# Router's GELU inside the attention loop, early logits and choices spread over group 7, the last four batches last

## The reference

```
x = x + tanh(g_xattn) * attention(layernorm(x), ctx)       # 16 heads of 16, causal
xf = layernorm(x); ri = concat(xf, six statistics of each row)
h = gelu(ri @ r1_w.T + r1_b); probs = softmax(h @ r2_w.T)  # 32 experts
top 2 of each token; each expert takes its 140 best tokens
x = x + tanh(g_ffn) * (experts' output, weighted + 16 shared adapters)
```

## Time and profile before

| | |
|---|---|
| median of 3 runs | 810.26 us (809.97 to 812.16) |
| profiled execution: its own time, its span | 806.49 us, 804.7 us |
| PE, DVE, ACT, POOL busy | 675.4, 507.6, 393.2, 322.9 us |
| mean granted PE clock | 0.914 of full |
| chain that ended last | PE 60%, DVE 17%, ACT 14% |

### The profile page before, as it was taken

How to read it: one execution, slowest core, us unless ns; L and a number is a source line. 1 busy time by engine, 2 the same in 40 slices (tenths; PEclk the granted TensorE clock), 3 DMA queues, 4 the chain that set the end, 5 groups by cost and what they waited for, 6 DMA issues and landing times.

```text
span 804.7 us, 17481 instructions
## 1 busy us (share of the span) xinstructions
PE 675.4 (84%) x5198; PEld 532.4 (66%) x5198; DVE 507.6 (63%) x1371; ACT 393.2 (49%) x1590; POOL 322.9 (40%) x339
## 2 busy tenths in 40 slices
PE   7899999999999999998866111079999999999993
PEld 4456666666666666665643100069999999999992
DVE  5665777867777786766578888925454545454541
ACT  1467686867768686777732563012222222222220
POOL 3343453534445353441101000035656565656542
PEclk8999999999999999999976555579999999999997
DMA  5600020202002020101014200018898988898931
GB/s 163 238 1 24 25 70 2 70 26 69 24 23 70 2 69 24 46 1 46 2 41 133 74 1 0 0 33 258 245 274 253 266 243 272 251 274 234 278 60 14
DMA packets 57422, 84.44 MB, mean 105 GB/s; under 512 B 11282, under 2 KB 28304, under 8 KB 57360
## 3 DMA queue, kind: packets, MB, share of 16 engines
q1 hardware_dynamic: 47168, 73.04, 27.7%
q0 software_dynamic: 9216, 9.76, 7.4%
q10 hardware_dynamic: 976, 0.96, 0.4%
HBM read 71.04 MB, written 12.69 MB: 104 GB/s over the span
## 4 chain that ended last, share of the span: by engine, by line
PE 60%; DVE 17%; ACT 14%; issue 4%; DMA 2%; SPq 1%; POOL 1%; ACTq 0%; DVEq 0%; POOLq 0%
PE pair L808 19%; PE bank L818 10%; ACT arena L1083 7%; PE pair L1385 6%; DVE arena L1254 5%; PE pair L1394 3%; PE bank L1413 3%; PE bank L1352 3%; PE pair L1380 3%; DVE arena L669 3%; PE bank L1340 2%; PE bank L1345 2%; PE bank L828 2%; ACT arena L489 2%; PE bank L1364 1%
## 5 line engine op out<-in xcount | busy, mean ns | idle before, releaser
L1083 ACT ACTIVATE arena<-pair,arena 112x112 f32<-112x112 f32 x512 | 175.5, 365 | 72.3 <-DVE arena L1254 68.5
L808 PE MATMUL pair<-arena,we 128*128 128x140 f32 x1024 | 139.9, 285 | 0.7 <-ACT arena L729 0.6
L772 DVE SCALAR_TENSOR_TENSOR arena<-arena,pair 128x140 f32<-128x140 f32 x160 | 47.7, 298 | 133.8 <-issue 73.6
L714 POOL DMA_INDIRECT rows_out<-arena,slot_row x64 | 94.4, 1475 | 92.7 <-DVE arena L761 75.0
L808 PEld LDWEIGHTS pair<-arena,we 128*128 128x128 f32 x1024 | 130.1, 192 | 1.8 <-issue 1.8
L737 ACT ACTIVATE arena<-pair 128x140 f32<-128x140 f32 x160 | 45.9, 287 | 149.0 <-PE pair L808 99.0
L705 POOL DMA_INDIRECT arena<-rows,slot_row x64 | 62.5, 977 | 120.8 <-issue 120.8
L1083 ACT ACTIVATION_READ_ACCUMULATOR arena<-pair,arena 112x1 f32 x512 | 110.0, 215 | 0.0
L818 PE MATMUL bank<-arena,we 128*128 128x140 f32 x512 | 83.3, 286 | 0.0
L1254 DVE TENSOR_REDUCE arena<-pair 112x8 f32<-112x896 f32 x64 | 69.4, 1085 | 19.8 <-PE pair L1385 19.0
L1394 PEld LDWEIGHTS pair<-tab,arena 112*112 112x112 f32 x512 | 52.0, 134 | 30.6 <-issue 28.7
(11 more groups left out here) (188 smaller groups left out, 1178.5 us busy)
## 6 DMA issues: line engine op xcount, KB each, us to landing
we<-w_experts_in SPq DMA_DIRECT2D x192, 256.0 KB
wa<-w_adapters_in SPq DMA_DIRECT2D x16, 384.0 KB
arena<-ctx_in SPq DMA_DIRECT2D x8, 448.0 KB, 4.4
arena<-x_in SPq DMA_DIRECT2D x8, 448.0 KB, 3.8
rows_out<-arena SPq DMA_DIRECT2D x8, 448.0 KB, 3.3
rows<-arena SPq DMA_DIRECT2D x8, 448.0 KB, 3.4
arena<-rows,slot_row POOLq DMA_INDIRECT x64
rows_out<-arena,slot_row POOLq DMA_INDIRECT x64
```

The lines of the kernel that those rows point to most:

```text
L714: nc.gpsimd.indirect_dma_start(d["out"], bass.IndirectOffsetOnAxis(ap=slot_row[:, h, e:e + 1], axis=0), yr[e % 2][:, h, :], None, compute_ ...
L772: signal(dve, nc.vector.scalar_tensor_tensor(gs[m % 2], th[m % 2], 1.0, banks[m % 4][:, 0:CAP], ALU.add, ALU.mult), s_gs, n + 1)
L808: last = nc.tensor.matmul(banks[m % 4][:, part * CAP:(part + 1) * CAP], w[:, col0:col0 + 128], xet[j % 2][:, c, :], start=(c == 0), stop=( ...
L1083: last = nc.scalar.activation(pr[s % 2][:, j, :], banks[BS[s % 4]][0:T, j * T:(j + 1) * T], ACT.Exp, bias=nmx[s // 2 % 2][:, s % 2, j:j + ...
```

## The change

- H writes `hpre` with `Gelu` in place of `Identity`, in the loop too; the separate GELUs go. In the tail a dummy activation at step 13 loads the GELU set ahead, and a dummy `Exp` behind H loads the Exp set.
- Logits of batches 0 to 15 go to steps 1 and 3 of group 7, of 16 to 23 to step 7, each ahead of the turning of the sums; of 24 to 27 to step 4 of the tail. `LATE` is four batches. Shifts, exps and choices are spread as the tables say.
- In the tail the two wide matmuls of H (448 columns) are issued at step 11 into another bank; the spare matmuls of step 12 are 12, not 18; those before the logits go.
- A column block of the scores is a batch's place in its run of eight, so blocks 0 to 3 are whole before the last choice: PE turns, ACT copies and DVE takes digit 0 by halves.
- Digits 1 and 2 (by halves) and the token weights (in 7 parts) stand one to a round. `srt` is loaded ahead of the expert pair. `max_index` looks only as far as the values sought. The last expert's two halves have a signal each.

```diff
@@ -40,7 +40,7 @@
...
 WARM = 12
-IDLE = {7: 12, 12: 18, 14: 2}
+IDLE = {7: 12, 12: 12, 14: 2}
@@ -167,18 +167,18 @@
-GELU, GELU_TAIL = 15, 5
-LOGITS = {16: (0, 1, 2, 3), 19: (4, 5)}
-EARLY_ROWS = (slice(0, 16), slice(16, 24))
-SHIFTED, RAISED = (17, 20), (18, 20)
+LOGITS = {1: (0, 1), 3: (2, 3), 7: (4, 5), 20: (6,)}
+EARLY_ROWS = (slice(0, 16), slice(16, 24), slice(24, 28))
+SHIFTED, RAISED = (3, 7, 22), (4, 8, 22)
 PARTS = 9
-CHOOSE = {19: ((0, 0), (0, 1), (0, 2)), 20: ((0, 3),), 21: ((0, 4), (0, 5)), 22: ((0, 6),), 23: ((0, 7),),
-          29: ((0, 8), (1, 0), (1, 1), (1, 2), (1, 3), (1, 4), (1, 5), (1, 6), (1, 7), (1, 8))}
-IDLE_LOGITS, WITH_LOGITS = 2, 0
-IDLE_LAST = {}
+CHOOSE = {5: ((0, 0), (0, 1)), 7: ((0, 2),), 9: ((0, 3), (0, 4)), 13: ((0, 5),), 15: ((0, 6), (1, 0), (1, 1)),
+          16: ((0, 7), (0, 8)), 18: ((1, 2),), 19: ((1, 3),), 20: ((1, 4),), 22: ((1, 5), (1, 6)),
+          29: ((1, 7), (1, 8)), 30: tuple((2, part) for part in range(PARTS))}
+HIDDEN_ROWS, HIDDEN_BANK = 11, 1
+TABLES = 13
@@ -474,11 +472,10 @@
...
         attention_done(act)
-        gelu(NG - 1)
-        shifted_exp(LATE, 3)
-        act.wait_ge(s_set, 1)
-        nc.scalar.copy(se[:, 0:GB * T], banks[2][:, 0:GB * T])
-        nc.scalar.copy(se[:, GB * T:], banks[3][:, 0:GB * T]).then_inc(s_set, 1)
+        shifted_exp(LATE, len(EARLY_ROWS) + 1)
+        for h in range(2):
+            act.wait_ge(s_set, h + 1)
+            nc.scalar.copy(se[:, h * GB * T:(h + 1) * GB * T], banks[2 + h][:, 0:GB * T]).then_inc(s_kept, 1)
@@ -503,11 +500,13 @@
...
-        pe.wait_ge(s_scr, 1)
         for j in range(CHB):
+            if j % GB == 0:
+                pe.wait_ge(s_scr, j // GB + 1)
...
                                        sc_flat[:, j * 128:(j + 1) * 128], ident[0:T, 0:T])
-        last.then_inc(s_set, 1)
+            if j % GB == GB - 1:
+                last.then_inc(s_set, 1)
@@ -595,24 +597,37 @@
...
         link(nc.vector.tensor_scalar(shift, tab[:, TAB["seek"]], -1.0, None, ALU.add))
-        shift_logits(dve, link, LATE, BS[0], EARLY // GB + 1)
+        shift_logits(dve, link, LATE, BS[0], NG)
         for part in range(PARTS):
-            choose(dve, link, LATE, part, 3)
+            choose(dve, link, LATE, part, len(EARLY_ROWS) + 1)
         dve.sem_inc(s_scr, 1)
-        token_weights(link, LATE)
+        def take_digit(k, h):
+            half_of = slice(h * GB * T, (h + 1) * GB * T)
+            shift = DBITS * (DIGITS - 1 - k)
+            link(nc.vector.tensor_scalar(digit_bits[k][:, half_of], se.bitcast(I32)[:, half_of], shift, (1 << DBITS) - 1,
+                                         ALU.logical_shift_right, ALU.bitwise_and))
+        def to_float(k, h):
+            half_of = slice(h * GB * T, (h + 1) * GB * T)
+            link(nc.vector.tensor_scalar(digit[k][:, half_of], digit_bits[k][:, half_of], 1.0, None, ALU.add))
+        def beside(n):
+            if n < 4 * (DIGITS - 1):
+                k, h = 1 + n // 4, n // 2 % 2
+                if n % 2 == 0:
+                    take_digit(k, h)
+                else:
+                    to_float(k, h)
+            else:
+                token_weights(link, n - 4 * (DIGITS - 1))
+        for h in range(2):
+            dve.wait_ge(s_kept, h + 1)
+            take_digit(0, h)
+            to_float(0, h)
         dve.wait_ge(s_dig, 16)
-        dve.wait_ge(s_set, 2)
-        def take_digit(k):
-            shift = DBITS * (DIGITS - 1 - k)
-            link(nc.vector.tensor_scalar(digit_bits[k], se.bitcast(I32), shift, (1 << DBITS) - 1,
-                                         ALU.logical_shift_right, ALU.bitwise_and))
-        def to_float(k):
-            link(nc.vector.tensor_scalar(digit[k], digit_bits[k], 1.0, None, ALU.add))
-        take_digit(0)
-        to_float(0)
@@ -631,10 +646,7 @@
...
                 last.then_inc(s_cnt, 1)
-                if k == 0 and r in (0, 1):
-                    take_digit(r + 1)
-                elif k == 0 and r in (2, 3):
-                    to_float(r - 1)
+                beside(ROUNDS * k + r)
@@ -666,7 +678,8 @@
...
             some = slice(i * FIND, (i + 1) * FIND)
-            last = nc.vector.max_index(at[:, some], place[:, CHB * T + i * FIND:CHB * T + (i + 1) * FIND], place)
+            end = CHB * T + (i + 1) * FIND
+            last = nc.vector.max_index(at[:, some], place[:, end - FIND:end], place[:, 0:end])
@@ -753,14 +768,15 @@
...
     def experts_vector(dve, link):
-        def turned(e, j):
+        def turned(e, j, halves=False):
...
                                                xr[j][:, h, bass.ds(C + e, 1)], None, ALU.mult)
-            last.then_inc(s_yr, 1)
+                if halves or h == 1:
+                    last.then_inc(s_yr, 1)
@@ -906,9 +922,9 @@
...
         attention_done(sp)
+        nc.sync.dma_start(srt, d["search"]).then_inc(s_dig, 16)
         load_pair(1, 1)
-        nc.sync.dma_start(srt, d["search"]).then_inc(s_dig, 16)
-        sp.wait_ge(s_wts, 2)
+        sp.wait_ge(s_wts, NCH)
@@ -1053,14 +1071,17 @@
...
                 act.wait_ge(s_fo, 16 * 2)
-                nc.scalar.activation(hpre[:, bass.ds(q * NT, NT)], src[:, 0:NT], ACT.Identity,
+                nc.scalar.activation(hpre[:, bass.ds(q * NT, NT)], src[:, 0:NT], ACT.Gelu,
                                      bias=r1b[:, 0:1]).then_inc(s_mf[kind], 1)
+                if tail:
+                    nc.scalar.activation(spare[:, 1:2], gates[:, 2:3], ACT.Exp)
...
                 if what not in "VO" and (what in "XTS" and s % 2 == 0) == early:
-                    item(g - back, (par + back) % 2, kind, what, j, n, front and not own)
+                    item(g - back, (par + back) % 2, kind, what, j, n, front and not own, not front and not own)
@@ -1095,24 +1116,21 @@
...
                                        banks[BO][:, 2 * T:4 * T]).then_inc(s_rdent, 1)
-                if own and not front and s == GELU:
-                    act.wait_ge(s_mf[2], FIRST[2] + len(ROUTE) * EARLY // GB)
-                    for early in range(EARLY // GB):
-                        gelu(early)
...
                     nc.scalar.activation(size, xf, ACT.Abs).then_inc(s_size, 1)
-                if not own and not front and s + STEPS in RAISED:
-                    h = RAISED.index(s + STEPS)
+                step = s if own else s + STEPS
+                if not front and step in RAISED:
+                    h = RAISED.index(step)
...
                     nc.scalar.activation(w0[:, rows, :], w0[:, rows, :], ACT.Exp).then_inc(s_e, 1)
-                if not own and not front and s == GELU_TAIL:
-                    act.wait_ge(s_mf[2], FIRST[2] + len(ROUTE) * (NG - 1))
-                    gelu(NG - 2)
+                if not own and not front and s == TABLES:
+                    nc.scalar.activation(spare[:, 0:1], gates[:, 2:3], ACT.Gelu)
@@ -1287,18 +1303,22 @@
...
                         rotate_all(z)
-                if not own and not front:
-                    if s + STEPS == SHIFTED[0]:
+                if own and not front:
+                    if s == SHIFTED[0]:
                         for done, value in ((s_v, 2 * NG), (s_proj, 4 * NG), (s_rope, 4 * NG), (s_xb, NG),
-                                            (s_xnt, 2 * NG), (s_kz, GB * g), (s_s, GU * g)):
+                                            (s_xnt, 2 * NG), (s_kz, GB * g + 1), (s_s, GU * g)):
                             dve.wait_ge(done, value)
-                    if s + STEPS in SHIFTED:
-                        rows = EARLY_ROWS[SHIFTED.index(s + STEPS)]
-                        shift_logits(dve, link, rows, BM[0], rows.stop // GB)
+                step = s if own else s + STEPS
+                if not front and step in SHIFTED:
+                    h = SHIFTED.index(step)
+                    rows = EARLY_ROWS[h]
+                    shift_logits(dve, link, rows, BM[0], rows.stop // GB, rows.start // GB % GB * GB * NE)
                 if not front:
-                    for h, part in CHOOSE.get(s if own else s + STEPS, ()):
+                    for h, part in CHOOSE.get(step, ()):
                         choose(dve, link, EARLY_ROWS[h], part, h + 1)
+                    if not own and s == STEPS - 1:
+                        dve.sem_inc(s_scr, 1)
@@ -1360,8 +1384,10 @@
...
                 wait(pe, s_xft, 3 * (q + 1))
-                for c in range(2):
-                    nc.tensor.matmul(out[:, 0:NT], r1t[:, c, :], xft[:, c, :], start=(c == 0), stop=False)
+                if tail:
+                    out = banks[BS[HIDDEN_BANK]]
+                else:
+                    hidden_rows(out)
@@ -1431,9 +1457,15 @@
...
-        def fill_in(times):
-            keep_warm(times, identb, causalb.unsqueeze(1).to_broadcast([T, HU, T]), BM[0])
+        def early_logits(early):
+            if early == 0:
+                pe.wait_ge(s_mf[0], len(FRONT) * NG)
+            elif early == GB:
+                pe.wait_ge(s_sub, 1)
+            elif early == NG - 2:
```

(30 more changed lines are left out.)

52 lines of the change are left out of this document (28 added, 24 removed).

## The result

| | before | after |
|---|---|---|
| median | 811.21 us of 4 runs (809.97 to 814.07) | 797.60 us of 4 runs (795.79 to 800.05) |
| profiled execution: own time, span | 806.49, 804.7 us | 796.95, 795.2 us |
| mean granted PE clock | 0.914 | 0.926 |
| PE, DVE, ACT, POOL busy | 675.4, 507.6, 393.2, 322.9 us | 667.8, 505.3, 407.6, 323.0 us |

The ratio of the medians is 0.984, 95% interval 0.982 to 0.986: 13.6 us faster on the same chip. The stages are compared on the traces; I cut them at DVE's maxima (L1254, now L1272), of which there are 64, 8 in each group.

A forecast was written before the change was run, and what follows sets the result against it. PE bounds the loop, a ring of waits group 7, a chain of short steps, mostly DVE, the tail. 2.0 + 5.6 - 20.9 - 0.3 - 1.3 - 0.4 = -15.3, from 810.26 to 795.0 us; range 792 to 799.

The forecast's parts named there:

- The loop, +2.0: Groups 1 to 6: two table loads around each H delay PE 0.4 us at five boundaries; 0 to +4.2 us.
- Group 7, +5.6: Last group: early logits, shifts, exps and choices put into its ring of waits lengthen it; +3 to +9.8 us.
- step 1: Group 7: logits of 8 batches stand where PE has hardly 0.3 us to spare; +1.7 us.
- step 3: Group 7: logits of 1.94 us against 1.19 us of idle time ahead of the sums; +0.75 us.
- steps 4 and 5: Group 7: exp of `w0` ahead of a copy PE awaits, +0.65 us; then DVE operations and a reciprocal, +0.15 us.
- step 7: Group 7: logits, shift and 16 MAX8 end at 376.3, past L1249 at 375.09; +1.2 us.
- step 13: Group 7: L1254 at 390.19 has no idle time ahead of it; +0.7 us.
- The tail, -20.9: Last exp to search: the search starts at 427.0, was 447.90; -24 to -15.8 us, depending on the clock.
- Finds -1.3 and end -0.4: `max_index` scans 972 columns on average, not 1040: -1.3 us; the last output's first DMA starts earlier: -0.4 us.
- Search, -0.3: Search rounds: DVE idles 0.4 us in each of 11, now each has 0.2 to 0.45 of work; -0.9 to +0.5 us.
- (a): Tail: the clock stays at half speed, 5.1 us less gained, 800.1 us; chance 0.17.
- (c): Loop switches: each load holds ACT as long again, 18.1 us more over six boundaries, 813.1 us; chance 0.04.

The follow-up runs named there:

- experiment 7: Changed kernel with the early logits, shifts, exps and choices of 24 batches put back from group 7 into the tail; 810.22 us, 0.999 to 1.002 of before.
- experiment 1: Changed kernel with Identity in place of Gelu in H in the loop, so no table load stands there; 793.24 us, 0.978 to 0.985 of before.
- experiment 6: Kernel before with one part of the change only: H writes Gelu, the separate GELUs go; 814.61 us, 1.004 to 1.008 of before.
- experiment 8: Kernel of experiment 3 plus 4 and 6 spare matmuls around the early logits in group 7; 791.36 us, 0.974 to 0.979 of before.
- experiment 3: Changed kernel with Identity in H in the loop and one GELU over 2688 columns at step 0 of group 7; 796.89 us, 0.983 to 0.990 of before.

## Why the prediction was right, and where it wasn't

The forecast was 795.0 us, measured were 797.6, by ratio 13.6 us gained for 15.3. The reason given, that the win is in the tail and the loop pays for it, is what the runs show: experiment 7 undoes the first and the whole gain goes, experiment 1 undoes the second and the loop is as before. That the number came so near is in part luck, as the end of this section tells. Term by term:

- **The loop, +2.0, was 8.45.** This is the term that was mis-sized, by four times. The step of it that failed is the price of a boundary, "0.4 us late with the hand-over". Its 0.84 from H with two loads and its 0.44 of slack are both in the trace. What it lacked are three pieces of 0.2 each: the load that waits behind the register wait (I took "it doesn't wait for data" from a load in straight code), H's own later start, and PE's start from idle; at a trip's end more (in experiment 6, which has no spell, two of the five boundaries cost 1.63 and 1.16 and the others 1.02 to 1.08). That makes 1.2 for 0.4. The load at the loop's entry (1.3) was not counted, nor the spell of half clock (some 1.2). The upper bound, +4.2, did not hold it. Experiment 1 gives the term as 8.6 with the spell, experiment 6 as 7.25 without one.
- **Group 7, +5.6, was 4.2** from maxima to maxima, 3.4 from H to H. In order of its steps: step 1 took 1.2 for the forecast 1.7 and step 3 0.3 for 0.75, as logits of 8 batches took 1.67 us and not 1.94 (the 3.88 us of the earlier trace rows that I halved ended at half clock: 0.54 on average from 400 to 402 us; in experiment 7 the same 32 matmuls took 3.24); steps 4 and 5 0.6 for 0.8, step 7 1.1 for 1.2, step 8 0.3 for 0.4, step 13 0.7 for 0.7. Nothing from the boundary, as forecast.
- **The tail, -20.9, was -18.8** from the last exp to the search (33.49 us for 52.25). The order of its events came as forecast. Counted from the last exp, forecast against trace: the copy of unit 15 at 1.95 and 1.83, the last residual 6.95 and 6.87, LN2 10.35 and 10.52, the wide matmuls 14.95 and 15.14, S 20.35 and 21.42, the last logits 23.45 and 24.93, the shift 24.45 and 25.98, the search 31.35 and 33.49. So it holds to 0.2 us up to the wide matmuls; these and the spare ones took 6.3 us for my 5.4, as the four ran at half clock throughout (3.35 us). The other misses are 0.4 around H and 0.6 from the shift on, in the hand-overs between the halves. DVE's "2 us of semaphores and set-up" are 2.46 and 0.8, and end as the logits do. That S waits for the spare matmuls was right and led nowhere: taking them out gains 0.3, as DVE ends last.
- **Finds -1.3 and end -0.4** came as forecast: the mean of 18 is 1163 ns for the forecast 1.16 us. **Search, -0.3**, was +0.2: DVE's idle time ahead of L651 fell from the 4.6 of the earlier trace rows to 2.6 us, and the rounds are no shorter; where that went I haven't followed. The experts took 1.6 us less in this pair of traces and from 266.9 to 270.0 us among the variants, which touch nothing there: scatter. For `srt` there is no wait, as forecast.
- **The rivals.** (a), half clock in the tail, is right in part: the clock is 0.82 on average from the last maxima on, and in the forecast's own loss of 2.1 us the wide matmuls at half clock are the largest piece. (c), dearer switches, is nearer than its 0.04 had it: a boundary lost 1.2, a little less than half of the 2.5 from which it decides. It supposed that each load holds ACT as long again, and no load does: H starts 1.29 us behind the start of its load, 1.28 of it the load. The drain of the Trainium skill ("ScalarE: Activation LUTs", What ACT_TABLE_LOAD costs) doesn't show at any of the 14 loads in and around the loop. The advice of the Trainium skill ("ScalarE: Activation LUTs", Table sets: the hidden batching unit) to batch calls by set agrees with experiment 8, which is 6 us better than the changed kernel; without the spare matmuls in PE's gaps (experiment 3) it gained nothing that the medians show.

The total came out nearer than its parts, by luck. The profiled execution was forecast at 791.2 and took 796.95: 6.5 us too little for the loop, 0.3 ahead of it, 1.5 too much of a gain from the last maxima to the search, 0.5 in the search, against 1.4 too much for group 7 and the 1.6 of scatter in the experts. The medians are closer, 795.0 and 797.6, because I had carried over 3.8 us between this execution and its median, and it was 0.65.

## What to carry to other kernels

A table load on an engine that "has room" is to be priced where it stands: what of that engine's work does the bounding engine wait for next, how long is the slack there, and does the load stand behind a wait or at a loop's entry. When work is put into a stage that PE bounds, price the gap that it makes by the clock that follows it; some spare matmuls in the gap can be worth more than the gap. And where all engines meet, choose what to wait for: a wait that is long fulfilled isn't always free.

## What the runs showed that I had not expected

- Two gaps of 0.73 and 1.15 us on PE, close together, were followed by 15 us at 0.50 of the clock while PE was busy all the time (experiment 3); with the gaps filled nothing fell (experiment 8). Gaps of this size don't always do it: in group 7 of the kernel before PE idles 1.19, 0.53 and 1.19 us in turn, at a clock of 1.00; in experiment 6, with 1.29, 1.19 and 1.20 us, it fell behind the second and the third.
- Short spells of half clock come and go between runs of nearly the same code. In the trace of experiment 8 the first 5 us of group 1 have a mean clock of 0.68, in that of 3 of 1.00, and group 1 takes 48.0 us and not 46.7. Such spells may be part of the 3 us and more by which runs of one kernel differ; only one run of each has a trace.

```profile
75.00:80.00 5.00, 5.00 (x30) 3.04 (x28) 3.71 (x11) 2.53 (x12) 0.23 (x1) 0.68 0.00 0
```

- With 34 fulfilled waits on semaphores taken out, DVE's gap behind a single short instruction was 2.00 us shorter, 59 ns each; only the gap shows them, put down to "issue" or to whatever came last. Behind 1.10 us of work in the kernel before the same 40 left a gap of 0.88 us.
- `FIND_INDEX8` took 1094 ns over 904 columns and 1233 over 1040: 8.2 ns for eight columns more.
